# Stores of all three bf16 parts ahead of the loads of the operand stacks

## The reference

```
x = x + attention1(layernorm(x))        # 16 heads of 16, layernorm of q and k per head, causal
x = x + ffn(layernorm(x))               # ffn = a second attention, then a mixture of experts
```

```
q = layernorm((x @ Wq.T) per head, gq, bq);  k likewise with gk, bk
scores = q @ k.T, causal;  attn = softmax(scores);  out = attn @ v @ Wo.T + bo
```

## Time and profile before

| | |
|---|---|
| median of 3 runs | 3575.92 us |
| the profiled execution's own time | 3571.57 us |
| its span | 3569.8 us |
| mean granted TensorE clock | 0.985 |
| TensorE busy | 3263.7 us, 91% |
| VectorE busy | 2760.8 us, 77% |
| ScalarE busy | 2136.2 us, 60% |
| loads of the stacks | 384, 128 KB each, median 5.2 us from issue to landing |
| stores of the parts | 192, 128 KB each, median 4.2 us from issue to landing |

### The profile page before, as it was taken

The page is one execution under the profiler, slowest core; times in us unless marked ns, Lnnn a source line. Parts: engine busy times, 40 slices in busy tenths (PEclk is TensorE's granted clock), DMA queues, the critical chain, the costliest instruction groups (busy, mean ns, idle before and its releaser), DMA issues.

```text
span 3569.8 us, 80003 instructions
## 1 busy us (share of the span) xinstructions
PE 3263.7 (91%) x30392; PEld 2602.3 (73%) x30392; DVE 2760.8 (77%) x5880; ACT 2136.2 (60%) x6105; POOL 960.0 (27%) x656
## 2 busy tenths in 40 slices
PE   3999999989999899998999999899998999989998
PEld 2777777777777777777777777777777777777777
DVE  5877878877787778778787787787887878777875
ACT  3666656566565665656665566665665656566663
POOL 3341232312323222232212323023230232312220
PEclk7999999999999999999999999999999999999999
DMA  6003030120302103030030300303002030110300
GB/s 137 7 1 60 7 60 7 22 45 2 60 7 40 28 2 60 7 56 12 1 60 8 60 7 4 58 7 60 8 17 51 2 60 7 34 34 2 60 1 7
DMA packets 74077, 104.33 MB, mean 29 GB/s; under 512 B 18464, under 2 KB 67488, under 8 KB 67552
## 3 DMA queue, kind: packets, MB, share of 16 engines
q1 hardware_dynamic: 73696, 99.23, 14.5%
HBM read 65.63 MB, written 33.55 MB: 28 GB/s over the span
## 4 chain that ended last, share of the span: by engine, by line
PE 55%; DVE 16%; ACT 12%; DMA 8%; issue 5%; SPq 3%; POOL 1%; ACTq 0%; POOLq 0%; DVEq 0%
PE bank L732 15%; PE bank L743 9%; ACT prob L1029 7%; DMA stash<-part 6%; PE scores L719 6%; PE scores L800 4%; PE scores L720 4%; PE scores L823 3%; PE scores L721 3%; SPq L470 2%; PE scores L849 2%; DMA qkt<-stash 2%; PE scores L713 2%; PE bank L676 2%; PE bank L836 1%
## 5 line engine op out<-in xcount | busy, mean ns | idle before, releaser
L1029 ACT ACTIVATE prob<-scores,negmax 128x128 f32<-128x128 f32 (+3 forms) x2048 | 1057.8, 536 | 263.2 <-DVE negmax L1297 252.7
L1297 DVE TENSOR_REDUCE negmax<-scores 128x1 f32<-128x128 f32 (+3 forms) x2048 | 873.5, 483 | 76.6 <-PE scores L721 62.7
L732 PE MATMUL bank<-ident,prob 128*128 128x128 f32 x5120 | 734.8, 281 | 65.0 <-DVE probt L1305 41.7
L1305 DVE COPY probt<-bank 128x512 f32<-128x512 f32 x896 | 596.8, 684 | 183.4 <-PE bank L732 177.8
L732 PEld LDWEIGHTS bank<-ident,prob 128*128 128x128 f32 x5120 | 552.1, 142 | 173.9 <-issue 73.8
L721 PE MATMUL scores<-mask,ident 128*128 128x128 bf16 x2048 | 440.2, 227 | 0.0
L1029 ACT ACTIVATION_READ_ACCUMULATOR prob<-scores,negmax 128x1 f32 x2048 | 436.3, 213 | 0.0
L719 PE MATMUL scores<-khh,qt 128*128 128x256 f32 (+2 forms) x1024 | 415.3, 406 | 13.2 <-POOL kll L605 13.2
L564 POOL TENSOR_TENSOR rq<-ssq,expo 128x32 f32<-128x32 f32 x64 | 363.1, 5692 | 75.7 <-DVE ssq L1269 50.7
L546 POOL COPY rexp<-rsum 128x512 f32<-128x512 f32 x128 | 78.1, 610 | 1094.6 <-DVE rsum L1309 1094.6
L551 POOL TENSOR_TENSOR otl<-onm,oth 128x512 fp32r<-128x512 f32 x96 | 122.7, 1278 | 881.8 <-ACT oth L974 881.8
(11 more groups left out here) (191 smaller groups left out, 6140.5 us busy)
## 6 DMA issues: line engine op xcount, KB each, us to landing
qkt<-stash SPq DMA_DIRECT2D x384, 128.0 KB, 5.2
stash<-part SPq DMA_DIRECT2D x192, 128.0 KB, 4.2
x_in<-in_x_rows SPq DMA_DIRECT2D x16, 512.0 KB, 4.0
out_rows<-x SPq DMA_DIRECT2D x16, 512.0 KB, 4.1
r_d<-in_wd SPq DMA_DIRECT2D x1, 1024.0 KB, 9.7
r_gu<-in_wg SPq DMA_DIRECT2D x2, 512.0 KB, 4.3
r_gu<-in_wu SPq DMA_DIRECT2D x2, 512.0 KB, 5.5
r_wob<-in_wo SPq DMA_DIRECT2D x4, 128.0 KB, 6.5
```

Source lines behind the costliest of these rows:

```text
L732: ins = nc.tensor.transpose(bank[4 + n % 2][:, q * P:(q + 1) * P], prob[:, u % 2, q, i * P:(i + 1) * P], ident[:, :])
L1029: nc.scalar.activation(prob[:, u % 2, q, 0:n], bank[q][:, 0:n], ACT.Exp, bias=negmax[:, a, u, q:q + 1], accum_out=sums[:, a, u, q:q + 1]). ...
L1297: nc.vector.tensor_reduce(negmax[:, a, u, M * part:M * part + M], scores[:, M * part:M * part + M, 0:n], axis=AX.X, op=ALU.max, negate=Tru ...
L1305: nc.vector.tensor_copy(probt[:, u % 2, i], bank[4 + n % 2][:, :]).then_inc(probt_dve.sem, 1)
```

## The change

Within `stack_rows`, the wait for the low part and its two stores move from behind the six loads of the high part to ahead of them. Nothing else changes: the number and size of the DMAs, the semaphores and their counts, and the instructions of the other four engines are the same.

```
             store_part(0, half, high_stored)
             sp.wait_ge(mid_ready.sem, mid_ready.at(b, 2 * half + 2))
             store_part(1, half, mid_stored)
+            sp.wait_ge(low_ready.sem, low_ready.at(b, 2 * half + 2))
+            store_part(2, half, low_stored)
             sp.wait_ge(high_stored.sem, high_stored.at(b, STORES * 16 * (half + 1)))
             load_slots(0, half)
-            sp.wait_ge(low_ready.sem, low_ready.at(b, 2 * half + 2))
-            store_part(2, half, low_stored)
             sp.wait_ge(mid_stored.sem, mid_stored.at(b, STORES * 16 * (half + 1)))
             load_slots(1, half)
             sp.wait_ge(low_stored.sem, low_stored.at(b, STORES * 16 * (half + 1)))
             load_slots(2, half)
```

## The result

| | before | after |
|---|---|---|
| median of four runs | 3574.93 us (3573.19 to 3580.74) | 3623.13 us (3620.72 to 3624.13) |
| profiled execution, its span | 3571.57, 3569.8 us | 3624.13, 3622.3 us |
| granted clock, mean of the span | 0.985 | 0.976 |

The ratio is 1.0133, with a 95% interval from 1.0119 to 1.0147. The changed kernel is 48 us slower; 28 us were forecast.

What follows compares the result with a forecast made beforehand. The bound was taken to be a full queue of stack loads on the DMA engines. Half 1's stack lands 2.95 - 2 x 0.66 = +1.6 us later, costing 16 + 11 + 1 = 28 us: 3604 us against the median 3575.92, range 3580 to 3625.

Steps and rivals of the forecast that it cites:

- The queue sets the end: Loads queue for the DMA engines, landing about 1 us apart; the queue is full from the first load, one gap between halves.
- The first rival: SP's waits, not the engines, set the end; all 38.5 us of load waits go, 3537 us against the median; chance 0.09.
- The high loads start 2.95 us later: Half 0's high loads now wait for the low part and the issue of its two stores: +2.95 us, uncovered.
- The low stores leave the streams, 0.66 us each: In each half's load stream, the two low stores no longer stand among the loads: -0.66 us per half.
- +1.6: Forecast shift in us of the landing of half 1's stack: 2.95 - 2 x 0.66.
- if nothing came back: Upper bound on the shift of half 1's stack, with no gain from stores leaving the streams: +2.95 us.
- Half 1's stores cost nothing extra: Half 1's stores queue behind half 0's loads as before; its low stores, now ahead of its loads, cost nothing there.
- 1.6 us in ten batches: In the ten batches that already wait, TensorE, and behind it ACT and DVE, wait 1.6 us longer: 16 us.
- Two of the signs: TensorE's load waits rise from 38.5 to about 60 us; ten batches take about 12.6 us from first transposes to fifth unit.
- 11 + 1 us in the other five: Four later batches with waits of some 1 us lose 2.8 us each, 11 us; the one without a wait loses 1 us.
- The rival "slower still": Waits of over 4 us keep the clock low for another stretch in all fifteen batches: 25 us more, 3629 us; chance 0.10.
- The prologue, 0: Ahead of the first batch, first scores come some 3 us later, hidden by DVE; half 1's loads between -0.7 and +0.7, taken as 0.

Runs made afterwards that it cites:

- Spread loads: Slot s of a stack on partitions s, s+6, s+12, ... instead of 16 neighbours: kernel before 3534.41 us (ratio 0.9898), changed kernel 3535.80 us (0.9898).
- early: Kernel before, with half 1's high and mid stores ahead of half 0's low loads and its low stores directly behind those: 3543.52 us, ratio 0.9916.

## Why the prediction was right in kind and too small in size

**The queue sets the end: right.** Landings are 0.97 us apart, half 1's stores queue behind half 0's loads, and once the loads no longer fill the queue, the order costs nothing. The first rival was to decide where a load takes the engines less than its issue. Spread loads, issued 0.63 us apart, reach that point, and both kernels with them came out at 3534 and 3536 us, where the rival's sum, all 38.5 us of waits gone, had 3537.

**The high loads start 2.95 us later: right.** Over the 15 batches the first load stands 7.44 us behind the first store instead of 4.64, +2.80.

**The low stores leave the streams, 0.66 us each: the first step that failed.** From its first load's issue to its last landing, half 0 takes 14.18 us instead of 14.45, -0.27, and half 1 14.22 instead of 14.16, +0.06 (means of 15). The gap between the halves is unchanged, 0.56 and 0.54. In place of +1.6 the shift is 36.40 - 33.78 = +2.6 us: my upper bound, "if nothing came back", was almost the value.

The gap that I read, 1.6 us from the sixth landing to the seventh, is no chance of one batch; its mean over the 15 is 1.62 in half 0 and 1.57 in half 1. What I left out is the step ahead of it. Before, the sixth load, the last one ahead of the stores, lands only 0.76 us after the fifth; after, with no stores behind it, 1.02 us. The rows are the fifth load of the batch of the earlier trace rows, issued at 2016.63, before, and the fifth to seventh, issued at 2051.16, 2051.62 and 2052.09, after; the sixth and seventh before are in the earlier trace rows, with 6.0 and 6.2:

```profile
qkt<-stash SPq DMA_DIRECT2D x1, 128.0 KB, 5.7
...
qkt<-stash SPq DMA_DIRECT2D x1, 128.0 KB, 5.4
...
qkt<-stash SPq DMA_DIRECT2D x1, 128.0 KB, 5.9
...
qkt<-stash SPq DMA_DIRECT2D x1, 128.0 KB, 6.4
```

From the fifth landing to the seventh that is 2.4 us before and 1.9 after. In the mean it is 2.38 and 2.02 us in half 0, 2.33 and 2.04 in half 1. So the stores cost the stream 0.36 and 0.29 us, not 0.66. The other landings lose 0.09 us of that again in half 0 and 0.35 in half 1, where the first load lands 0.15 us later after its issue; why was not tried.

A single pair of batches misleads as well: from 2010.19 and 2041.85 to the stacks of these two batches the difference is only +1.9, since half 0 alone moves by some 0.4 us from batch to batch.

**Half 1's stores cost nothing extra: nearly right,** by the unchanged gap; the 0.15 us above may be theirs.

**1.6 us in ten batches: too small.** They lose 2.93 us each: 2.2 by the wait and 0.7 because the clock stays low for longer behind it. Their sum is 29.3 instead of 16 us. Two of the signs that I named are missed in size likewise: TensorE's waits for the loads are 91.4 us in total, not about 60, and the ten batches take some 14.2 us to the fifth score unit, not 12.6.

**11 + 1 us in the other five: the larger miss.** They lose 5.98 us each, 29.9 together. I gave them the wait of the others. But in four of the five the waits had been short for a reason that I had not seen: the last matmuls of the experts ran slowly, so the first transposes came 32.2 us behind the first store instead of 30.7, and the stack, at its usual 33.8, was nearly in time. (In the fifth, and in one of the four, the stack itself came early, at 32.2 and 32.3.) The rows are two windows ahead of an attention, before and after:

```profile
722.00:733.05 11.05, 8.55 (x59) 7.66 (x57) 4.92 (x11) 4.65 (x12) 0.00 (x0) 0.85 1.02 155
```

```profile
2062.00:2072.55 10.55, 8.06 (x62) 6.98 (x62) 5.04 (x12) 4.65 (x12) 0.00 (x0) 1.00 0.94 180
```

After, only one batch still has such a stretch, and these 1.5 us of cover are gone. The five now wait as long as the ten: the third unit moves by 4.1 us and the slow clock adds 1.9.

**The rival "slower still" had half of it.** It gave 3629 us from waits of over 4 us and a further slow stretch in all fifteen batches. The waits came, 3.9 to 5.8 us. The clock's added cost is 10 x 0.7 + 5 x 1.9 = 16.5 us of the 59, where the rival had 25; the longer waits are 10 x 2.2 + 5 x 4.1 = 42.5. By its time the result is nearer to this rival than to the forecast, and I gave it 0.10.

**The prologue, 0: nearly right.** TensorE ahead of the first batch, against the earlier trace rows:

```profile
68.13 0.26 PE L713 MATMUL scores<-qkt 96*128 96x128 bf16 x1 [6.60 <-DMA qkt<-stash]
...
82.37 0.40 PE L713 MATMUL scores<-qkt 96*128 96x256 bf16 x1 [10.12 <-DMA qkt<-stash]
```

The first scores come 3.4 us later (3 were forecast), the wait for the stores at 77.63 is gone, and the third unit comes 0.5 us earlier.

## What to carry to other kernels

Compare how far apart transfers land with how far apart they are issued. Where they land further apart, an order of issue can only start the full queue earlier or later (the change) or close a gap in it (early), and the shape of the transfer matters first: spread partitions took 37 us off the old order and some 85 off the new.

Price a wait of TensorE with the slow stretch behind it, and ask of each batch that does not wait what kept it from waiting. Read what a transfer costs in a stream from the steps on both sides of it, against the same steps without it: the gap alone gave 0.66 us, both steps 0.36 and 0.29.

## What the runs showed of the hardware

A load of 128 KB onto 16 neighbouring partitions takes the queue about 1.0 us (the median distance of landings before; 131072 bytes / 1.0 us = 131 GB/s). Onto 16 partitions that are 6 apart, loads land 0.67 us apart (median), about as SP issues them (0.63), with the DMA engines at 0.60. SP takes 0.59 us to issue such a load instead of 0.42.

The Trainium skill bears on it: "SBUF — State Buffer", section "Door 1: The DMA port swizzle (why `[64,N]` ≈ `[32,N]`)", says that DMA bandwidth goes by how many of the memory's 16 ports the partitions reach. By its table the 16 neighbours reach 4 ports, the spread ones 13 or 14, and 4/16 of its 436 GB/s give an estimate of 1.2 us for a load, against 1.0 us measured. The direction agrees, and the measured time is the shorter; no run here tells the ports apart from another effect of neighbouring partitions.

After a wait of 4.5 us TensorE worked for 5.9 us at 1.2 GHz, at a cost of about 2 us; with unused matmuls in the wait the clock stayed at 2.4 GHz. Matmuls put into one idle place can move the fall to another.

Now and then a single issue by SP takes 1.0 to 1.6 us, where 0.42 is usual: 11 of the 360 loads of the changed kernel's later batches, as 1.36 us for the second load of half 1 at 2063.79. What holds it was not tried.
